# Last expert layer: a second shared-expert group computed ahead of the block loop, six instead of seven beside the gathering of results

## The reference

```python
x = x + jnp.tanh(g_ffn[3]) * _L3_ffn_ref(_layernorm(x, axis=-1), ...)

def _L3_ffn_ref(x, router_w, router_bias, gate_w, up_w, down_w, sgate_w, sup_w, sdown_w):
    TOPK = 4
    ...
    topk_scores, topk_idx = jax.lax.top_k(scores, TOPK)
    ...
    h = silu(flat @ gate_w[e]) * (flat @ up_w[e]); expert_out = h @ down_w[e]
    out = (sel * topk_scores[:, :, None]).sum(axis=1)
    out = out + jax.nn.silu(flat @ sgate_w.T) * (flat @ sup_w.T) @ sdown_w.T
```

## Time and profile before

| what | us |
|---|---|
| median of 3 runs | 4259.48 (4255.28 to 4262.33) |
| the profiled execution's own time | 4255.14 |
| its span | 4253.4 |
| stage D in it, from its first instructions to the end | 3759.8 to 4253.4 |
| first loop matmul | 3789.9 |
| first and last gather of results | 4056.79, 4246.86 |

### The profile page before, as it was taken

One profiled execution on the slowest core, in us unless ns is written; L12 is line 12 of the kernel. 1 busy time (PEld: TensorE's weight loads), 2 busy tenths in 40 slices (PEclk: granted clock), 3 DMA queues, 4 the chain that ended last, 5 costly groups with the idle time before them and its releaser, 6 DMA issues. The chain is left out here.

```text
span 4253.4 us, 77426 instructions
## 1 busy us (share of the span) xinstructions
PE 3971.4 (93%) x28880; PEld 2796.9 (66%) x28960; DVE 2250.9 (53%) x6853; ACT 1746.0 (41%) x3685; POOL 1066.0 (25%) x1239
## 2 busy tenths in 40 slices
PE   7999999999999999999998899999998898789987
PEld 4666666666666666666665489976666565468854
DVE  4555665566556555655564521136766665344444
ACT  4445554555455545554542111113544444313310
POOL 2221222122212221222120011111022222245555
PEclk9999999999999999999999999999999898899998
DMA  3003303330333033303310169960212111159934
GB/s 116 2 12 117 116 10 110 117 116 9 110 117 117 11 108 117 117 11 108 115 58 28 75 233 333 334 212 28 66 61 70 60 55 47 43 199 321 322 117 131
DMA packets 285453, 472.83 MB, mean 111 GB/s; under 512 B 23009, under 2 KB 224609, under 8 KB 276513
## 3 DMA queue, kind: packets, MB, share of 16 engines
q1 hardware_dynamic: 227632, 371.88, 25.8%
q0 software_dynamic: 24480, 66.88, 5.1%
q10 hardware_dynamic: 32976, 29.13, 2.0%
HBM read 266.74 MB, written 201.06 MB: 110 GB/s over the span
## 5 line engine op out<-in xcount | busy, mean ns | idle before, releaser
L496 POOL TENSOR_SCALAR a_wide_p<-a_wide_p,a_w_inv 128x512 f32<-128x512 f32 x512 | 356.7, 710 | 1440.3 <-DVE a_w_inv L1164 1440.3
L938 ACT ACTIVATE a_wide_p<-a_wide_p,a_row_min 128x512 f32<-128x512 f32 x512 | 363.6, 713 | 120.5 <-DVE a_row_min L1159 120.3
L1234 DVE TENSOR_REDUCE a_q_pad<-ring 128x4 f32<-128x1024 f32 x256 | 302.3, 1219 | 76.2 <-PE ring L720 76.2
L580 PE MATMUL ring<-a_qk 64*128 64x512 f32 x678 | 288.1, 641 | 19.1 <-ACT a_wide_pt L967 12.2
L1159 DVE CUSTOM_DVE_ANT_0 a_wide_p<-ring,a_neg_keys 128x512 f32<-128x512 f32 x339 | 226.9, 688 | 116.3 <-PE ring L580 115.8
L995 ACT ACTIVATE a_probs<-ring 128x1024 f32<-128x1024 f32 x256 | 251.1, 1022 | 82.1 <-PE ring L734 82.1
L2803 DVE CUSTOM_DVE_ANT_0 shared_w<-ring,c_neg_mask 128x256 f32<-128x256 f32 x512 | 186.4, 421 | 138.8 <-remote 82.2
L1689 PE MATMUL ring<-b_xgt,b_we 128*128 128x128 f32 x2016 | 235.5, 275 | 0.5 <-DVE b_xgt L1879 0.5
L1689 PEld LDWEIGHTS ring<-b_xgt,b_we 128*128 128x128 f32 x2016 | 230.2, 192 | 0.8 <-DVE b_xgt L1879 0.7
L2612 ACT ACTIVATE c_probs<-ring 128x1024 f32<-128x1024 f32 x128 | 131.0, 1024 | 223.5 <-PE ring L2358 176.2
L580 PE MATMUL acc<-a_qk 64*128 64x512 f32 x346 | 194.6, 642 | 8.5 <-ACT a_wide_pt L967 5.0
(11 more groups left out here) (459 smaller groups left out, 8677.1 us busy)
## 6 DMA issues: line engine op xcount, KB each, us to landing
d_cells<-a_neg_keys SPq DMA_DIRECT2D x66, 2048.0 KB, 16.2
b_we<-in_experts SPq DMA_DIRECT2D x63, 1536.0 KB
d_we<-in_experts SPq DMA_DIRECT2D x159, 256.0 KB
d_results<-d_yb ACTq DMA_DIRECT2D x159, 128.0 KB
a_k_t<-in_ctx_keys SPq DMA_DIRECT2D x16, 512.0 KB
a_v_pad<-in_ctx_values SPq DMA_DIRECT2D x16, 512.0 KB
c_k_t<-in_ctx_keys SPq DMA_DIRECT2D x16, 512.0 KB, 3.6
c_v_pad<-in_ctx_values SPq DMA_DIRECT2D x16, 512.0 KB, 3.5
```

Source lines behind the costliest of these rows:

```text
L496: ins = pool.tensor_scalar(wide_p[:, h % 4, t, :], wide_p[:, h % 4, t, :], w_inv[:, t, h:h + 1], 1.0, ALU.mult, ALU.mult)
L580: pe.matmul(wbank(name), qk[u % 2][64 * j:64 * j + 64, t * P:(t + 1) * P], qk[u % 2][64 * j:64 * j + 64, 256:768], start=True, stop=True). ...
L938: ins = act.activation(wide_p[:, h % 4, t, :], wide_p[:, h % 4, t, :], ACT.Exp, scale=-1.0, bias=row_min[:, h, t:t + 1], accum_out=row_sum ...
L1234: dve.tensor_reduce(q_pad[:, :, 2 * i:2 * i + 2, HD].rearrange("p t h -> p h t"), s, AX.X, ALU.max, negate=True).then_inc(nr.taken(name), 1)
```

## The change

`early` becomes 2. PE computes group 1 ahead of the loop too: its four `shared_in` stand between the `shared_out` of group 0, and its four `shared_out` behind them. DVE has the `shared_hidden` of group 1 between the adds of group 0, and then the adds of group 1. ACT's list follows `early` by itself (four more silus ahead of the loop). After the loop the groups 2 to 7 are left beside the gathering.

```diff
                         if finish:
                             for i in range(4):
+                                shared_in(first + 1, i)
                                 shared_out(4 * first + i)
+                            for i in range(4):
+                                shared_out(4 * first + 4 + i)
                             pe.wait_ge(downs_loaded, 16)
                             pe.wait_ge(experts_ready, 1)
...
                             for n in range(4):
+                                shared_hidden(4 * first + 4 + n)
                                 shared_add(4 * first + n)
+                            for n in range(4):
+                                shared_add(4 * first + 4 + n)
...
-            expert_layer(rd, 128, gates[:, 7:8], a["experts3"], 0, 1, True)
+            expert_layer(rd, 128, gates[:, 7:8], a["experts3"], 0, 2, True)
```

## The result

The changed kernel takes 4276.64 us (median of 19 runs, 4265.38 to 4287.12), the kernel before 4257.91 (19 runs beside them, 4246.17 to 4271.62). The ratio is 1.0043, 95% interval 1.0033 to 1.0053. By the medians that is +18.7 us. The sum had +16.0, the forecast was 4275. The profiled execution of the changed kernel took 4265.38 us, span 4263.6, the shortest of its 19.

A forecast was written before the change was run, and what follows sets the result against it. PE without a gap bounds the opening, PE and DMA are near full in the loop, POOL's gathers set the gathering's end. 20.6 + 0.8 - 5.4 = +16.0 us on the median 4259.48 gives 4275, range 4264 to 4283.

The forecast's parts named there:

- Opening, +20.6: Ahead of the loop: four more shared_in and shared_out cost PE their full 20.6 us, bounds 19 and 22.
- Loop, 0: Loop: same order and same full buffers at its start, so its length does not change, 0 us.
- rival C: Loop: transfers get ahead of a later PE and up to 17.2 us come back, 4258.3 us; chance 0.05.
- Load of group 3, +0.8: Loop's end: this load now shares the DMA engines with the last gathers, 0 to 1.7 us, middle +0.8.
- Gathering, -5.4: Gathering of results: the two pauses of the last part go, -5.4 us, bounds 0 and 28.7.
- A sign of being wrong: Gathering: the forecast is wrong if the pauses in the first 96 results come in other places.
- rival A: Gathering: nothing comes back, the pauses only get other places; +21.4 us, 4280.9 us; chance 0.20.
- Rival B: Gathering: one to three more pauses go, some 5 us each, about 4266; chance 0.14, its limit 4252.2 gets 0.04.
- The own time: Whole kernel: the profiled execution's 4255.14 plus 16.0 gives 4271.1 us.

The follow-up runs named there:

- lot 2: Batch of follow-up kernels on one chip of its own, with the kernel before beside them at 4214.65 us (27 runs).
- lot 3: Batch of follow-up kernels on another chip of its own, with the kernel before beside them at 4215.31 us (29 runs).
- front_filler: The kernel before with 131 instead of 40 unread matmuls ahead of the first shared_out, nothing taken from beside the gathering; 4113.63 us, ratio 1.0040.
- gather_alone: The kernel before with groups 1 to 7 left out of all engines, so no shared work beside the gathering; 4206.67 us, ratio 0.9983.
- lot 1: Batch of follow-up kernels on a chip without real gathering pauses, with the kernel before beside them at 4094.75 us (22 runs).
- yk16_again: The kernel before with 16 instead of 8 buffers for gathered results, run in lot 3; 4221.21 us, ratio 1.0010.
- table_yk16: The kernel before without the 40 unread matmuls, DVE's result-slot table spread over loop blocks 40 to 72, 16 result buffers; 4214.95 us, ratio 0.9999.
- changed_again: The changed kernel itself, run again in lot 2; 4233.53 us, ratio 1.0044 to the kernel before.
- changed_yk16: The changed kernel with 16 instead of 8 buffers for gathered results; 4238.32 us, ratio 1.0057 to the kernel before.
- yk4: The kernel before with 4 instead of 8 buffers for gathered results; 4212.92 us, ratio 0.9998.
- table_in_loop: The kernel before without the 40 unread matmuls and with DVE's result-slot table spread over loop blocks 40 to 72; 4213.06 us, ratio 0.9991.
- none_ahead: As table_in_loop, but no group ahead of the loop, all eight beside the gathering, 70 unread matmuls in the opening; 4220.30 us, ratio 1.0011.
- yk16: The kernel before with 16 instead of 8 buffers for gathered results, run in lot 1; 4094.90 us, ratio 0.9998.

## Why the prediction came out right, and where it was off

The measured 4276.64 lies 1.6 us from the forecast of 4275. Part of that closeness is luck: the cost by the medians was 18.7 where the sum had 16.0, and the kernel before was 1.6 us faster in the nineteen runs (4257.91) than in the three that the forecast started from (4259.48). By its terms:

- **Opening, +20.6:** measured +20.6 here, 51.8 - 31.2 = 20.6 in lot 2, and 51.9 - 31.2 = 20.7 in lot 3. PE was what everything waited for, and pure PE filler costs as much (front_filler).
- **Loop, 0:** +0.3, and +0.3 with the filler. In the other pairs with one group more ahead it is -1.2 (lot 3), +2.3 (lot 2, against gather_alone) and +2.4 (lot 1, without the filler). Loops of kernels that do the same in the loop differ by up to 2.9 us within a lot, so this is no clear cost, and nowhere do the up to 17.2 us of rival C come back. Rival C falls. Its price was misread from the start: it called 17.2 us of the loop waits, for transfers in the main, but PE is busy for 255.61 of the 261 us of the old loop, and waits for gathers for only 1.9 of them.
- **Load of group 3, +0.8:** the way from the loop to the first gather is 0.9 longer in the first pair, 0.8 in lot 3 and 1.5 in lot 2, but no longer in lot 1 (4.7 with either number of groups). Ahead of its first gather POOL now waits 14.2 us for the store of the last results, and 12.6 in the kernel before. In the first pair that is the middle I had taken; over the lots the cost lies anywhere between 0 and 1.5. By the Trainium skill ("DMA: Bandwidth & Descriptors", section "Queues, rings and completion order") each engine takes turns between the queues that have work. By that some of the 1.7 us of the load falls on the last stores and gathers; the trace of the first pair, with 0.9 us, agrees with it, lot 1 shows no such cost, and no run shows the turns themselves.
- **Gathering, -5.4:** the mechanism held, and the size was a little large. Up to the 97th gather there are six pauses as before, 1.3 us longer in sum, and the pauses ahead of the 113th and 114th are gone. They stayed with 28 pairs and 16 buffers (4.79 and 1.74 in yk16_again, 2.96 and 1.74 in table_yk16), and are gone with 24 pairs (the last pause is ahead of the 97th gather here, and of the 101st in changed_again and in changed_yk16, both with 24 pairs). Two kernels with 28 pairs have their last pause elsewhere: yk4 ahead of the 109th (4.14), table_in_loop ahead of the 105th (3.15), the latter with an end that is 3.8 us longer. With 24 pairs no kernel has a pause behind the 101st, and with 32 pairs (none_ahead) the last one stands ahead of the 125th. So the last pause follows the number of pairs, 97 to 101 with 24, 105 to 114 with 28, 125 with 32, and the last pauses do hang on the group that is no longer there. The table of lot 2 alone would not show this: 101 against 105. On the chip of lot 1, where no pauses stood, nothing came back: 160.4 against 160.3.
- **A sign of being wrong came up.** The prediction called itself wrong if the pauses in the first 96 results came in other places. Two of them did, by four gathers each (69 for 65, 81 for 85), and three changed by over 1 us (3.29 to 2.22, 3.20 to 5.63, 4.72 to 5.76). Number and sum stayed, so the total held; that the old course comes back pause by pause did not. POOL's waits for DVE came to 31.0 us, where about 30 were expected.
- **How much comes back** is known less well. The profiles give -4.6 here and -5.2 in lot 3, but kernels with 28 pairs lie between 185.2 and 190.1 us among themselves (mean of five 187.1), those with 24 between 183.6 and 185.5 (mean of three 184.3), which is -2.8. The medians leave, from the +21.4 of the other terms, 21.4 - 18.7 = 2.7, 21.4 - 18.9 = 2.5 and 21.4 - 17.1 = 4.3 us, but -1.6 in lot 3 if the changed kernel is set against the kernel before with 8 buffers. So it is some 2 to 5 us, between the forecast and rival A. By the medians rival A isn't refused: the interval of the first ratio is 14.1 to 22.6 us and holds its 21.4. Against it stand the shorter gathering of the profiles and the place of the last pause. Its "nothing" is seen in lot 1. Rival B, that more pauses go, found nothing for it.
- **The own time** of the profiled execution (4265.4 against the 4271 of the sum) missed for a reason outside the sum: stages A to C differed by 7.0 us between the two executions. The median was the right thing to lean on.

What stays open is why PE's products are taken late in the first pair and in lots 2 and 3, and not in lot 1. No kernel paused POOL on purpose, which would have tested the length of a run by itself. In lot 2 the gathering grows with the pairs beside it, 159.3 us with none, 183.7 with 24, 185.3 with 28 and 188.2 with 32, but among kernels with 28 pairs the spread of one profile to the next is as large as the step of one group.

## What to carry to other kernels

Work moved from a stage with slack into one where a single engine has no gap costs its whole duration there; look in the profile for who waits for that engine at the border (here a gather waiting 10.49 us) before counting on cover. What comes back at the place it left is only what that stage's own bound gives up, and if that is a sum of irregular pauses, one profile tells it to no better than several microseconds: price it low, and lean on medians. And an unread filler can be free because it stands over another engine's hole: the filler taken out alone gained nothing here. The filler and the hole (DVE's table) taken out together made the front 7.2 us shorter, but the median moved by only 1.6 us, since the table cost time in the loop.

## What the runs showed of the hardware

One and the same kernel took 4257.91, 4094.75, 4214.65 and 4215.31 us in the first pair and the three lots. Between the profiles of the kernel before and of yk16 in lot 1 (spans 4253.4 and 4093.4) 122.9 us of the difference lie in stages A to C, 9.7 in the loop and 29.9 in the gathering of results. That stretch, kernels with the same work beside the gathers (8, 16 and 4 buffers), first of the kernel before, then yk16 in lot 1, then yk4 in lot 3:

```profile
4057.00:4247.00 190.00, 154.44 (x441) 89.57 (x439) 85.91 (x181) 16.40 (x28) 122.18 (x128) 0.90 0.41 122
```

```profile
3927.00:4087.00 160.00, 143.85 (x441) 84.06 (x439) 88.43 (x181) 16.72 (x28) 121.31 (x128) 0.98 0.48 145
```

```profile
4022.00:4207.00 185.00, 152.29 (x441) 88.65 (x439) 87.50 (x181) 16.70 (x28) 120.80 (x127) 0.92 0.42 125
```

The same 441 PE records and 128 gathers (one of them just outside the third window) take 160 us where the granted clock of the stretch is 0.98, and 185 to 190 where it is 0.92 and 0.90. The lower clock need not be the cause: PE has 26.1 us of waits (19.5, 3.6 and 3.0, by what ended them) in the stretch of the kernel before and 8.5 us in that of lot 1 (4.4 and 4.1), and the clock falls behind such waits. From 4175 to 4180 in the kernel before PE has nothing to do; the granted clock of 4170 to 4175 is 1.00, that of 4180 to 4185 0.50, the lower of its two levels, and from 4190 on it is 1.00 again. In the long runs between pauses PE is seen to stall without anything that it waits for, and ACT to take a product long after it. The timeline of the changed kernel, 34 us into the gathering:

```profile
4105.74 0.59 PE L1632 MATMUL ring<-shared_x,shared_w 128*128 128x512 f32 x1 [0.90 <-issue]
...
4107.86 0.59 PE L1632 MATMUL ring<-shared_x,shared_w 128*128 128x512 f32 x1 [1.53 <-issue]
...
4109.29 0.59 PE L1632 MATMUL ring<-shared_x,shared_w 128*128 128x512 f32 x1 [0.84 <-issue]
...
4111.43 1.09 ACT L1739 ACTIVATE d_shared_sil<-ring 128x512 f32<-128x512 f32 x2 [24.97 <-DMA shared_w<-in_shared]
```

ACT had been idle for 24.97 us, and the name behind its wait, a load of stage A, can't be what it waited for. What holds these two engines up was not found.
